# Combining the routed experts' rows inside the second attention's pipeline instead of ahead of it, with the second attention's weights loaded during the expert phase

## The reference, cut to what matters

```python
x = x + tanh(g_xattn[0]) * attention_0(layernorm(x), ctx, ctx, ...)
x = x + tanh(g_ffn[0])   * moe(layernorm(x))
x = x + tanh(g_xattn[1]) * attention_1(layernorm(x), ctx, ctx, mask, ...)
x = x + tanh(g_ffn[1])   * quantised_ffn(layernorm(x))

# moe: y = sum over the 2 chosen experts of 8 of weight * mlp_e(x); z = mlp_shared(x); y + z
# attention_1: 16 heads of width 64
q = split_heads(Q @ W_q + b_q); k = split_heads(K @ W_k + b_k); v = split_heads(V @ W_v + b_v)
scores = where(mask == 0, -1e9, q @ k.T / 8)
out = softmax(scores) @ v            # per head
out = out.transpose(...).reshape(..., 1024) @ W_o + b_o
```

## Time and profile before

| | us |
|---|---|
| median of 3 runs | 2545.97 |
| the 3 runs | 2545.56 to 2551.55 |
| the profiled execution, its own time | 2544.37 |
| span of the profiled execution | 2542.7 |
| PE busy in the span | 1931.0 (76%) |
| DVE, ACT, POOL busy | 1595.6, 1112.6, 832.0 |

### The profile page before, as it was taken

The page is one execution under the profiler, slowest core; times in us unless marked ns, Lnnn a source line. Parts: engine busy times, 40 slices in busy tenths (PEclk is TensorE's granted clock), DMA queues, the critical chain, the costliest instruction groups (busy, mean ns, idle before and its releaser), DMA issues. The chain is left out here.

```text
span 2542.7 us, 48798 instructions
## 1 busy us (share of the span) xinstructions
PE 1931.0 (76%) x14975; PEld 1392.6 (55%) x14984; DVE 1595.6 (63%) x3248; ACT 1112.6 (44%) x2555; POOL 832.0 (33%) x1334
## 2 busy tenths in 40 slices
PE   1898898998804794399999008999999999995275
PEld 1576676676503463166666006777777777773122
DVE  5777777777466542144444544677667667666797
ACT  1354454454443221022222104667667666664363
POOL 2000000000000233322221656667667667662004
PEclk9799999999955897699999559999999999998598
DMA  3000000000062000011111423223223222321001
GB/s 100 9 6 7 8 4 8 8 4 4 1 220 69 1 0 1 24 56 56 56 56 48 138 75 84 68 54 82 68 52 76 68 60 63 72 59 35 0 0 66
DMA packets 91445, 118.64 MB, mean 47 GB/s; under 512 B 18200, under 2 KB 60840, under 8 KB 91304
## 3 DMA queue, kind: packets, MB, share of 16 engines
q1 hardware_dynamic: 82728, 98.93, 14.2%
q0 software_dynamic: 8576, 17.87, 2.5%
HBM read 56.92 MB, written 17.90 MB: 29 GB/s over the span
## 5 line engine op out<-in xcount | busy, mean ns | idle before, releaser
L912 POOL TENSOR_SCALAR a_P<-a_P,a_RS 128x256 f32<-128x256 f32 x512 | 249.1, 487 | 191.6 <-DVE a_RS L1148 157.7
L1080 ACT ACTIVATE a_P<-a_pS,a_NM 128x256 f32<-128x256 f32 x512 | 238.0, 473 | 85.7 <-DVE a_NM L1144 85.1
L504 PE MATMUL a_pT<-a_Q,a_K 128*128 128x256 f32 x1024 | 243.3, 383 | 8.5 <-ACT a_PT L587 8.5
L1144 DVE TENSOR_REDUCE a_NM<-a_pS 128x2 f32<-128x512 f32 x256 | 175.5, 686 | 117.4 <-PE a_pS L995 117.4
L587 ACT ACTIVATE a_PT<-a_pT 128x512 f32<-128x512 f32 x256 | 151.2, 597 | 187.7 <-PE a_pT L504 187.4
L1089 ACT ACTIVATE a_PH<-a_pT 128x512 f16<-128x512 f32 x256 | 153.6, 600 | 131.4 <-PE a_pT L1003 120.8
L504 PEld LDWEIGHTS a_pT<-a_Q,a_K 128*128 128x128 f32 x1024 | 183.6, 190 | 39.0 <-ACT a_PT L587 16.4
L1154 DVE TENSOR_TENSOR a_PL<-a_pT,a_PH 128x512 f16<-128x512 f32 x256 | 174.8, 683 | 43.0 <-ACT a_PH L1089 41.8
L420 POOL TENSOR_TENSOR a_cl<-a_ctxin,a_ch 128x512 f16<-128x512 f32 x16 | 18.5, 1158 | 542.8 <-ACT a_ch L557 542.8
L694 DVE TENSOR_REDUCE a_M<-a_pS 128x2 f32<-128x512 f32 x256 | 163.0, 683 | 32.7 <-PE a_pS L483 32.1
L1003 PE MATMUL a_pT<-g_ident,a_P 128*128 128x128 f32 x1024 | 154.3, 274 | 7.3 <-DVE a_PL L1154 3.4
(11 more groups left out here) (411 smaller groups left out, 5625.9 us busy)
## 6 DMA issues: line engine op xcount, KB each, us to landing
a_KD<-a_KN SPq DMA_DIRECT2D x128, 128.0 KB, 2.4
a_QS<-a_QN SPq DMA_DIRECT2D x128, 128.0 KB, 2.3
we_stage<-mw SPq DMA_DIRECT2D x24, 512.0 KB, 4.6
ys<-me_yb SPq DMA_DIRECT2D x72, 128.0 KB, 1.7
a_ctxin<-ctxT SPq DMA_DIRECT2D x32, 256.0 KB, 2.7
a_KZ<-a_KN SPq DMA_DIRECT2D x64, 128.0 KB, 2.4
g_X<-x SPq DMA_DIRECT2D x1, 4096.0 KB, 14.8
rows<-mr_row SPq DMA_DIRECT2D x32, 128.0 KB, 1.7
```

The lines of the kernel that those rows point to most:

```text
L504: last = nc.tensor.matmul(pT[h % 2][:, kt, :], K32[par][h % 2][:, h // 2, kt * P:(kt + 1) * P], Q32[par][:, h // 2, :], start=True, stop=True)
L912: last = nc.gpsimd.tensor_scalar(P32[u % 4][:, a, :], P32[u % 4][:, a, :], RS[u % 4][:, a:a + 1], LIFT, ALU.mult, ALU.mult)
L1080: last = nc.scalar.activation(P32[u % 4][:, a, :], pS[u % 2][:, a, :], ACT.Exp, bias=NM[u % 4][:, a:a + 1], accum_out=SM[u % 4][:, a:a + 1])
L1144: nc.vector.tensor_reduce(NM[u % 4][:], pS[u % 2][:], AX.X, ALU.max, negate=True).then_inc(s_max.sem, 1)
```

## The change

1. The 64 fetches, the additions and the statistics leave the serial stretch. A new plan `comb(b, par, turn)` does batch b's share two steps ahead of its back: on POOL in turn 8 four small copies and four indirect transfers, and in turn 13 a power; on DVE in turn 12 four additions, two statistics, two aggregations and a small add, and in turn 15 four small operations. Batch 0 is done alone before the first front, batch 1 beside it, batches 2 to 15 in the 14 steps that follow.
2. The serial `load_split` of the four weights goes. The weights are loaded and split in eight halves (512 KB each) during the expert phase: ACT issues the transfer and makes the high half, POOL the low half, after every eighth tile. Their place is that of XT, which the routed phase no longer reads. The loops of ACT and POOL there are cut into nine.
3. The four clearings of KZ move from DVE in the serial stretch to POOL at the start of the attention.
4. `layernorm_stats` ahead of the second attention goes.
5. The banks pF[0] and pF[1] swap roles from batch to batch. The transposes of the tokens wait for the last but one value piece, and the wait for the last one goes to the first key product behind them.
6. The loop over steps has one turn less, and two more steps stand outside it.

```diff
-    with ExitStack() as c2:
-        on_pool, add_share = moe_combine(nc, c2, X, *combine)
-        ...
-        load_split(nc, c2, "w1", [(w_d[n].rearrange("(k p) n -> p k n", p=P), W[n][0][:], W[n][1][:]) for n in "qkvo"], KD * INNER, beside)
-    with ExitStack() as c2:
-        layernorm_stats(nc, c2, "l2", X, combine[0], mean, rstd)
...
+        run(UNITS, comb(0, 0, 0))
+        run(UNITS, now(front(0, 0)), comb(1, 1, 0))
+        step(back(0, 0), idle, later(front(0, 0)), now(front(1, 1)), comb(2, 0, 1))
+        with eng.Fori(0, B // 2 - 2) as i:
+            b = i * 2 + 1
+            step(back(b, 1), back(b - 1, 0), later(front(b, 1)), now(front(b + 1, 0)), comb(b + 2, 1, i + 1))
+            step(back(b + 1, 0), back(b, 1), later(front(b + 1, 0)), now(front(b + 2, 1)), comb(b + 3, 0, i + 2))
...
+    GATHER, ADD, ROOT, REFINE = 8, 12, 13, 15
...
+            nc.gpsimd.memset(half[:], -0.5).then_inc(cleared, 1)
+            pool.wait_ge(cleared, 1)
+            for z in (z for zs in KZ for z in zs):
+                nc.gpsimd.memset(z[64:P, :, :], 0.0).then_inc(cleared, 1)
+            pool.wait_ge(cleared, 5)
+
+            def comb(b, par, turn):
+                def gathers():
+                    if not isinstance(b, int) or b > 1:
+                        combined.wait(pool, b, -1)
+                    for q in range(2 * TOPK):
+                        nc.gpsimd.tensor_copy(pick[par][q][:], POS[:, q % TOPK, bass.ds(2 * b + q // TOPK, 1)]).then_inc(pick_ready.sem, 1)
+                    pick_ready.wait(pool, b, 4)
+                    nc.gpsimd.nop(nofuse=True)
+                    for q in range(2 * TOPK):
+                        nc.gpsimd.indirect_dma_start(out=routed[par][q][:], out_offset=None, in_=y_d,
+                                                     in_offset=bass.IndirectOffsetOnAxis(ap=pick[par][q][:], axis=0)).then_inc(gathered[par].sem, 16)
+
+                def inverse_root():
+                    var_ready.wait(pool, b, 1)
+                    nc.gpsimd.nop(nofuse=True)
+                    nc.gpsimd.tensor_tensor(root[:], var[:], half[:], ALU.pow).then_inc(root_ready.sem, 1)
+                return plan((GATHER, gathers), (ROOT, inverse_root))
...
                     xn_ready.wait(pe, b, 1)
-                    v_lo.wait(pe, b, 0)
+                    if not isinstance(b, int) or b:
+                        v_lo.wait(pe, b, -1)
...
                         if q == 0:
                             ctx_lo.wait(pe, b, 1)
+                            v_lo.wait(pe, b, 0)
...
+                def add():
+                    comb_steps.begin(b)
+                    gathered[par].wait(dve, turn, 64)
+                    for k in range(TOPK):
+                        for j in range(2):
+                            x = X[:, bass.ds(2 * b + j, 1), :].rearrange("p a d -> p (a d)")
+                            last = nc.vector.scalar_tensor_tensor(x, routed[par][TOPK * j + k][:], GW[:, k, bass.ds(2 * b + j, 1)], x, ALU.mult, ALU.add)
+                        link(last)
+                    nc.vector.nop(nofuse=True)
+                    for j in range(2):
+                        last = nc.vector.bn_stats(bn[:, j, :], X[:, bass.ds(2 * b + j, 1), :].rearrange("p a d -> p (a d)"))
+                    last.then_inc(combined.sem, 1)
+                    combined.wait(dve, b, 1)
+                    nc.vector.nop(nofuse=True)
+                    for j in range(2):
+                        last = nc.vector.bn_aggr(moments[par][:, j, :], bn[:, j, :])
+                    link(last)
+                    nc.vector.tensor_scalar(var[:], moments[par][:, :, 1], EPS, None, ALU.add).then_inc(var_ready.sem, 1)
+
+                def finish():
+                    root_ready.wait(dve, b, 1)
+                    link(nc.vector.tensor_tensor(corr[:], root[:], root[:], ALU.mult))
+                    link(nc.vector.tensor_tensor(corr[:], corr[:], var[:], ALU.mult))
+                    link(nc.vector.tensor_scalar(corr[:], corr[:], -0.5, 1.5, ALU.mult, ALU.add))
+                    link(nc.vector.tensor_tensor(rstd[par][:], root[:], corr[:], ALU.mult))
+                    comb_steps.end()
+                return plan((ADD, add), (REFINE, finish))
...
+                def next_low(j):
+                    pool.wait_ge(next_hi, j + 1)
+                    nc.gpsimd.tensor_tensor(columns(j, 1), stage[j % 2][:], columns(j, 0), ALU.subtract).then_inc(next_lo, 1)
...
+            def next_high(j):
+                if j >= 1 and j + 1 < AHEAD:
+                    act.wait_ge(next_lo, j)
+                    next_load(nc.scalar, j + 1)
+                act.wait_ge(staged[j % 2], 16 * (j // 2 + 1))
+                nc.scalar.activation(columns(j, 0), stage[j % 2][:], ACT.Copy).then_inc(next_hi, 1)
```

More of the change, by code:

```diff
@@ L793, in attention1 @@
     f_full = s.counter("f_full", 13)
+    pick_ready, gathered = s.counter("pick_ready", 4), [s.counter(f"gathered{i}", 64, start=0) for i in range(2)]
+    combined, var_ready, root_ready = s.counter("combined", 1), s.counter("var_ready", 1), s.counter("root_ready", 1)
+    comb_steps = s.chain("comb_steps", 7)
     k_flat, q_flat = s.counter("k_flat", 4), s.counter("q_flat", 4)
@@ L825, in now, with batches, step @@
         return {t: p[t] for t in p if t < UNITS}
-    def batches(eng, front, back):
-        def step(new, old, soon):
+    def batches(eng, comb, front, back):
+        def step(new, old, *soon):
             (new_low, new_first), (old_low, old_first) = new, old
@@ L834, in batches, with uncombined @@
         idle = ({}, {})
[L835 to L842 removed]
+        run(UNITS, comb(0, 0, 0))
[5 more added lines that the diff above has]
+            step(back(b + 1, 0), back(b, 1), later(front(b + 1, 0)), now(front(b + 2, 1)), comb(b + 3, 0, i + 2))
+        step(back(B - 3, 1), back(B - 4, 0), later(front(B - 3, 1)), now(front(B - 2, 0)), comb(B - 1, 1, B // 2 - 1))
+        step(back(B - 2, 0), back(B - 3, 1), later(front(B - 2, 0)), now(front(B - 1, 1)))
+        step(back(B - 1, 1), back(B - 2, 0), later(front(B - 1, 1)))
+        step(idle, back(B - 1, 1))
+    def uncombined(b, par, turn):
+        return {}
+    GATHER, ADD, ROOT, REFINE = 8, 12, 13, 15
     with nc.Block() as block:
@@ L1035, in back @@
                             *[(2 * p2 + LAG_OUT, lambda p2=p2: project(p2)) for p2 in range(PAIRS)]), {}
-            batches(pe, front, back)
+            batches(pe, uncombined, front, back)
         @block.scalar
@@ L1097, in back @@
                         plan(*[(u, lambda u=u: exps(u)) for u in range(UNITS)]))
-            batches(act, front, back)
+            batches(act, uncombined, front, back)
         @block.vector
@@ L1529, in _ @@
                     gather(q, q)
-                with pool.Fori(1, n // 4) as i:
-                    for q in range(4):
-                        xt_full.wait(pool, i * 4, q - 3)
-                        gather(i * 4 + q, q)
+                for j, (i0, i1) in enumerate(SPANS):
+                    with pool.Fori(i0, i1) as i:
+                        for q in range(4):
+                            xt_full.wait(pool, i * 4, q - 3)
+                            gather(i * 4 + q, q)
+                    if j < AHEAD:
+                        next_low(j)
             @block.sync
@@ L1616, in step @@
                 nc.scalar.activation(hh[:].rearrange("p k t -> p (k t)"), pH[:], ACT.Copy).then_inc(hh_ready.sem, 1)
-            steps_of(act, n, step)
+            def next_high(j):
[4 more added lines that the diff above has]
+                nc.scalar.activation(columns(j, 0), stage[j % 2][:], ACT.Copy).then_inc(next_hi, 1)
+            if ahead:
+                next_load(nc.scalar, 0)
+                next_load(nc.scalar, 1)
+                step(0, 0, lambda d: d // 4, True, False)
+                for j, (i0, i1) in enumerate(SPANS):
+                    with act.Fori(i0 - 1, i1 - 1) as i:
+                        for u in range(1, 5):
+                            step(i * 4 + u, u % 4, lambda d: i + (u + d) // 4, False, False)
+                    if j < AHEAD:
+                        next_high(j)
+                for st in range(n - 3, n):
+                    step(st, st % 4, lambda d: (st + d) // 4, False, st == n - 1)
+            else:
+                steps_of(act, n, step)
         @block.vector
```

126 lines of the change are left out of this document (50 added, 76 removed).

## The result

| | before | after |
|---|---|---|
| median of 7 runs each | 2547.14 us | 2559.34 us (2556.98 to 2564.16) |
| ratio, 95% interval | | 1.0048 (1.0036 to 1.006) |
| a second comparison, medians of 18 and 11 runs | 2546.06 us | 2557.85 us, 1.0045 (1.0028 to 1.0061) |
| profiled execution, span | 2544.37, 2542.7 us | 2562.53, 2560.5 us |
| a second profile of each, span | 2543.7 us | 2546.9 us |

The forecast was 2537 us. The range held the time; the direction was wrong.

A forecast was written before the change was run, and what follows sets the result against it. It took the serial stretch to cost its whole length and the second attention to be bound by PE. Terms: 2544.4 - 112.1 + 16.5 + 88.2 - 3.4 + 2 = 2535.6; median 2537 us, range 2505 to 2570.

The forecast's parts named there:

- serial stretch: Between the expert phase and the second attention, where PE does nothing: its removal gives back 112.1 us.
- start of the attention: Clearings and batch 0's share delay the first transposes by 9.9 us, batch 1's fetches add the rest: +16.5 us (14 to 21).
- 14 steps, with the clock's -3.4: Batches 2 to 15 at 6.3 us per step, +88.2 us, with -3.4 for fewer stretches at low clock.
- The step, POOL: Turn 8: a block of 6.1 to 6.2 us makes PE wait 4.0 us at unit 8: +5.3 us per step.
- The step, DVE: Turns 12 and 15: 4.7 us of work less 3.6 slack, arriving at the last value piece: +1.1 us per step.
- the port rival: POOL and DVE hold each other up; additions stretch by 0.4 us each, up to 1.7 us a step: 2554 us, chance 0.08.
- The step, turn 2: Four token transposes run under the wait for the last value piece: gain 0.5 us per step, at most 1.9.
- The clock: Low clock behind PE's wait at unit 8: +0.4 us per step; fewer slow stretches after the 1.9 us waits: -3.4 in all.
- Low clock in every step: Rival: low clock outlasts the wait for unit 9, 1.9 to 3.0 us per step: 2558 to 2573 us, chance 0.24.
- The fetches fit: Rival: POOL's margin at units 8 and 9 becomes 3 us or more: 2495 us, chance 0.12.
- Experts' fetch starves: Rival: the expert phase's fetch starves behind POOL's subtraction: +13, so 2550 us, chance 0.06.
- Gain and price cancel: Rival: steps cost 6.4 to 7.4 us more each: 2539 to 2553 us, chance 0.18.

The follow-up runs named there:

- the spread kernel: Changed kernel with a batch's four fetches issued in four turns (14 and 15 of the step before, 0 and 1 of its own), not one block: 2454.35 us, 0.9662.
- half a dose: Changed kernel with two of a batch's four fetches moved to turns 14 and 15 of the step before, two left in turn 8: 2491.0 us, 0.9808.
- the experiment with the banks: Kernel before with only the two F banks alternating by the batch's parity: 2536.09 against 2542.3 us, 0.9979.
- third profile: Changed kernel run once more, unchanged, for its ratio: 1.0045; span of its profile 2561.2 us.
- the filler: Changed kernel with 16 products of 512 columns, result overwritten, ahead of PE's transposes of unit 8: 2548.87 us, 1.0032.

## Why the prediction was wrong, by its steps

It forecast 2535.6 us for the profiled execution; that came to 2562.5, 26.9 more. The stages give (first pair of profiles, us; another 0.3 lies between span and time):

| term | forecast | measured |
|---|---|---|
| serial stretch | -112.1 | -112.1 |
| start of the attention | +16.5 | +20.4 |
| 14 steps, with the clock's -3.4 | +84.8 | +92.6 |
| expert phase | +2 | -0.7 |
| tail of the attention | 0 | +2.1 |
| before the experts | 0 | +6.4 (second pair +4.2) |
| stage behind the attention | 0 | +9.1 (second pair -2.3) |

**Serial stretch and start.** After, POOL starts the attention at 1413.04, 4.0 us behind the start of the experts' last product, as SP did before. The second batch's transposes come 58.0 us later (1471.01), before it was 149.7: 91.7 saved, forecast 95.6. The first batch cost +11.3 (forecast 9.9), the second +9.2 (6.6). POOL's power, of which no row existed, took 0.73 us, not 0.5.

**The step, POOL: right.** Block 6.2 us, measured 6.3; wait 4.0, measured 3.85; price 5.3, measured 5.6 in plain steps (53.9 against the spread kernel's 48.3), with half a dose near the same rule. The margin read from the earlier trace rows was the most useful number of the whole prediction.

**The step, DVE: wrong in place.** The forecast 1.1 us a step was for DVE's whole share, late for the last value piece. The additions alone cost 1.0 on average, but some 2 us in a step with the jump and 0.4 in a plain one, and all that the spread share costs in a plain step is 0.4. They are also stretched, as the port rival had it, by less than its 0.4 us: 0.63 us, and 0.72 for the first of a batch, against 0.488, the group rows after:

```profile
L1152 DVE SCALAR_TENSOR_TENSOR g_X<-a_routed,g_GW,g_X 128x256 f32 x48 | 28.2, 628 | 1.8 <-DVE g_X L1152 1.8
L1152 DVE SCALAR_TENSOR_TENSOR g_X<-a_routed,g_GW,g_X 128x256 f32<-128x256 f32 x16 | 10.8, 715 | 13.8 <-DMA a_routed<-ys,a_pick 13.6
```

**The step, turn 2: right in sum by luck.** 0.5 us a step forecast for hidden transposes; 0.1 came. The 5 to 6 us of the whole kernel came from the clock, as the experiment with the banks shows.

**The clock: wrong in both places.** 0.4 us in each step was too much for a plain one with a single stretch at half clock, where the filler shows nothing. And the -3.4 was for half of the low stretches behind the 1.9 us waits. With the banks alternating all of them went, 1.6 us each, but in the changed kernel new ones came behind the wait for POOL and at the jump: a granted clock of 0.96 and, in the third profile, 0.94, where it was 0.99. The Trainium skill ("TensorE: Matmul & The Clock Gate", why this matters for your kernels) warns against gaps between bursts of matmuls. The low clock did follow the gaps here; it cost nothing in a plain step with one such stretch, where POOL was the bound, and 1.6 us in the kernel before, where PE was.

**The plain step came out near by luck in its parts.** Against before's 48.0 us it is about 5.9 us dearer, forecast 6.3: POOL 5.6 (5.3), everything else 0.4 (1.1 for DVE and 0.4 for the clock), turn 2 -0.1 (-0.5).

**The step that failed** is the multiplication, "Fourteen steps carry a share (batches 2 to 15): +88.2 us". It took all steps as like the one in the earlier trace rows, a plain one, and put the jump at nothing. Five steps hold the loop's jump. Step by step against the kernel before, these five cost 47.3 us more in sum, 9.5 each, and the nine plain ones 45.3, 5.0 each. The forecast has 6.06 for every step with its share of the -3.4: 30.3 for the five and 54.5 for the nine. It was 17.0 us short at the jump and 9.2 over elsewhere. That its sum for the steps was still only 7.8 us off is luck: five plain steps of before were longer already, by a low clock that costs nothing in the changed kernel's plain steps.

What made the jump dearer is known in part. Without the jump a step of the spread kernel loses its 3.6 us, so the jump is the place. Leaving out most of the additions takes 2 us off a step with the jump. That DVE's refinement, the last work ahead of its own jump, does the rest is argued from the gaps at one jump and not shown.

The stages that the change touches sum to +11.1 over the forecast. That would make 2546.7, some 2 us slower than before. The rest of the 26.9 lies ahead of the experts (6.4) and in the last stage (9.1), which the forecast put at nothing and where profiles of one kernel differ by as much. The prediction said that its 6.3 us stood close to the 6.9 that decide, and a sum of five estimates multiplied by 14 could not carry a direction at that distance.

**The rivals.** Low clock in every step: there, but free where it came once in a plain step; it cost up to 1.3 us where it lasted twice as long. Port hold-up: there, 0.14 to 0.23 us an addition. The token normalisation that the prediction quotes for it reads one tile of tokens, not two, so it is weak evidence for a hold-up of instructions with two inputs. The fetches fit: not in turn 8; spread over four turns they do. Experts' fetch starves: not seen, 334.2 us for 334.9 between the experts' first and last transposes. Gain and price cancel: that is nearest to what happened, by another sum.

**The move itself is worth 86 us.** Spread over four turns it runs in 2454.35 us against 2539.82 for the kernel before in the same comparison. With four steps to a trip, it runs in 2441.31 us against 2542.3, 101 less.

## What to carry to other kernels

Work moved into a pipeline on a second engine cost its longest unbroken piece less the margin of the next result that the bound engine needs, not its sum. Read that margin at the place, and cut the piece to fit it: in turn 8 the whole block of fetches cost 83 us and more in 14 steps over its four parts, and the four parts with all the rest 0.4 us a plain step. Before multiplying a step's price, list the steps that are unlike the others, the loop's jump first. Before moving work within a queue, name the next instruction behind it that somebody waits for. When a forecast comes out right, look whether its mechanism did: the bank alternation earned its microseconds from the clock, not from the overlap.

## What the hardware showed beyond that

- The jump of the loop holds up more than one engine. In the spread kernel PE was idle 1.9 to 2.8 us there and ACT 1.7 us at two of them, with no releaser in the profile or one that by the kernel is none, and DVE took up its next maximum 1.26 us late. A step with it took 51.6 to 52.5 us, without it 48.4, and 51.6 and 51.8 also where the clock stayed at 1.00.
- A stretch at the low clock costs what its engine's bound allows: 1.6 us a step in the kernel before (49.6 for 48.0), nothing in a plain step of the changed kernel behind the wait for POOL (53.9 us with the clock low in after, and with it at 1.00 under the filler).
- After 3.85 us of idle time PE's clock is down at once (transposes of 0.60 us take 1.11), and it is back to 0.89 on average in 1838 to 1842. With the gap filled by useless products, down to an idle time of 0.38 us, it stays at 1.00.
- PE's wait of 1.92 us for the last value piece was followed by the low clock in four of 13 steps of one profile of before and in six of 13 of the other, the wait of 1.48 us with the banks alternating in none of 13.
- A power of 2 elements on each of 128 partitions takes POOL 0.73 us, more than a copy of 128x512 (0.61).
